# One front program for layer norm, gates and context keys and values, and the spread of the keys moved into the output product

## The reference

```python
x = x + attn(layernorm(x))              # gated delta rule, 16 heads of 128
x = x + xattn(layernorm(x), ctx)        # cross attention to 4 x 64 context rows, 16 heads of 32
x = x + ffn(layernorm(x))               # self attention and two of eight experts
```

```python
# attn: gates of every token and head
g    = exp(-exp(A_log) * softplus(x @ Wa.T + dt_bias));   beta = sigmoid(x @ Wb.T)
# ... recurrence over the tokens, RMS norm, gate by silu(x @ Wg.T), then
out  = o @ Wo.T
# xattn: all 256 context rows serve as keys and values of all queries
kv   = cond @ Wkv + bkv;   k, v = kv[:, :, 0], kv[:, :, 1]
k    = _fq_sym(k, axis=-1)      # rounded to 127 steps of the largest of each key and head
v    = _fq_sym(v, axis=2)       # rounded to 127 steps of the largest of each column
attn = _fq_unsigned(softmax(q @ k.T));   out = (attn @ v) @ Wp + bp
```

## Time and profile before

| what | us |
|---|---|
| median of 3 runs | 3815.62 (3815.4 to 3816.27) |
| the profiled execution, its own time | 3817.35 |
| its span, from first to last instruction | 3815.6 |
| PE busy | 3332.3 (87%) |
| DVE busy | 2142.5 (56%) |
| ACT busy | 1866.6 (49%) |
| POOL busy | 1576.9 (41%) |

### The profile page before, as it was taken

One profiled execution on the slowest core, in us unless ns is written; L12 is line 12 of the kernel. 1 busy time (PEld: TensorE's weight loads), 2 busy tenths in 40 slices (PEclk: granted clock), 3 DMA queues, 4 the chain that ended last, 5 costly groups with the idle time before them and its releaser, 6 DMA issues. The chain is left out here.

```text
span 3815.6 us, 61633 instructions
## 1 busy us (share of the span) xinstructions
PE 3332.3 (87%) x19300; PEld 2601.2 (68%) x19300; DVE 2142.5 (56%) x4562; ACT 1866.6 (49%) x4568; POOL 1576.9 (41%) x3055
## 2 busy tenths in 40 slices
PE   3699999999999999997993888699979999964993
PEld 1588888888888888886772444488746666653441
DVE  3476677666767776765225777555354654621223
ACT  2467776777677766774111555344343533530110
POOL 2577777777777777773001000255530000003103
PEclk7799999999999999998996999899989999975996
DMA  2222222222222222223344000133362022044325
GB/s 51 78 63 67 70 54 70 62 70 65 65 66 71 65 62 70 69 52 100 116 127 169 9 14 14 51 104 110 102 244 89 11 77 71 16 146 156 119 94 157
DMA packets 432119, 311.55 MB, mean 82 GB/s; under 512 B 131392, under 2 KB 348608, under 8 KB 430816
## 3 DMA queue, kind: packets, MB, share of 16 engines
q1 hardware_dynamic: 424544, 288.99, 25.4%
q0 software_dynamic: 5120, 16.78, 1.4%
q10 hardware_dynamic: 2304, 4.20, 0.3%
HBM read 195.99 MB, written 113.90 MB: 81 GB/s over the span
## 5 line engine op out<-in xcount | busy, mean ns | idle before, releaser
L534 PE MATMUL gd_PJ<-xn_lead,gd_w_rest 128*128 128x512 f32 x1024 | 421.4, 411 | 0.0
L534 PE MATMUL gd_PJ<-xn_lead,gd_w_lead 128*128 128x512 f32 x1024 | 403.0, 394 | 0.0
L534 PE MATMUL gd_PJ<-xn_rest,gd_w_lead 128*128 128x512 f32 x1024 | 401.3, 392 | 0.0
L977 POOL TENSOR_TENSOR gd_T<-gd_T,gd_prod 32x14 f32<-32x14 f32 (+6 forms) x896 | 314.2, 351 | 70.2
L974 POOL TENSOR_TENSOR gd_prod<-gd_L,gd_T 32x14 f32<-32x14 f32 (+6 forms) x896 | 285.2, 318 | 70.2
L699 DVE SCALAR_TENSOR_TENSOR gd_conv<-gd_pre,gd_cur_a,gd_conv 128x512 f32<-128x512 f32 x384 | 301.7, 786 | 9.1 <-ACT gd_conv L858 2.3
L2523 POOL MEMSET ms_rank<- 128x1 f32 x8 | 0.3, 98 | 559.2 <-POOLq L55 559.2
L534 PEld LDWEIGHTS gd_PJ<-xn_lead,gd_w_lead 128*128 128x128 f32 x1024 | 193.4, 189 | 43.8
L534 PEld LDWEIGHTS gd_PJ<-xn_lead,gd_w_rest 128*128 128x128 f32 x1024 | 194.2, 190 | 37.4
L534 PEld LDWEIGHTS gd_PJ<-xn_rest,gd_w_lead 128*128 128x128 f32 x1024 | 194.5, 190 | 35.3
L2297 ACT ACTIVATE sa_E<-sa_B,sa_nmax 128x512 f32<-128x512 f32 (+3 forms) x256 | 132.4, 525 | 151.5 <-DVE sa_nmax L2347 151.5
(11 more groups left out here) (403 smaller groups left out, 8905.7 us busy)
## 6 DMA issues: line engine op xcount, KB each, us to landing
turned_queries_keys<-f_wq SPq DMA_DIRECT2D x16, 1280.0 KB, 6.0
gd_row_sums<-decay_sums SPq DMA_DIRECT2D x64, 256.0 KB, 3.7
triangles<-gd_Lo SPq DMA_DIRECT2D x64, 256.0 KB, 3.4
gd_W<-turned_image SPq DMA_DIRECT2D x64, 256.0 KB, 2.8
gd_T<-inverse_image SPq DMA_DIRECT2D x64, 256.0 KB, 3.3
gated_outputs<-gd_og SPq DMA_DIRECT2D x64, 256.0 KB, 2.7
go_ogt<-gated_outputs SPq DMA_DIRECT2D x16, 1024.0 KB, 6.8
sa_qT<-turned_queries_keys SPq DMA_DIRECT2D x16, 1024.0 KB, 5.6
```

The costliest lines, as they stand in the source:

```text
L534: mm = pe.matmul(bank, w_parts[wp][:, j, k, :], rhs, start=(k == 0 and wp == 1), stop=(k == KT - 1 and wp + xp == 0))
L977: nc.gpsimd.tensor_tensor(T16[:, rows, 0:j], T16[:, rows, 0:j], prod[:, rows, 0:j], ALU.subtract).then_inc(solving, 1)
```

## The change

1. `front` takes the place of the layer norm and gates blocks: one block. Tiles of x, the normalised tiles and statistics are double (`xt[:, b % 2]`). The products of the gates, their transposes, the context's transposes, the key product and the value products are put between the transposes of x in PE's list. DVE takes the gates of batch b-1 after normalising batch b, then rounds the keys, then the last gates, then the values. ScalarE copies the turned context after batch 2. SP loads also the context, Wkv in two halves, its biases and the first head's weights `wraw`. Rounded keys `kf`, value integers `vi` and value scales `vs` stay in SBUF through the head stage.
2. `delta_heads` loads only three blocks of 128 constant columns, and no first weights.
3. `delta_out` turns keys and values on PE before it turns Wo. POOL sets `kbd` to zero, spreads the three parts of the keys and scales Wp. Wp and Wq are loaded behind Wo.
4. `cross_setup` becomes `cross_stats`: loads of x first, statistics of each batch as it lands, two biases.

The core of the diff:

```diff
-        xt = sb("xt", [P, CH, DIM])
+        xt = sb("xt", [P, 2, CH, DIM])
...
+            load_x(0)
+            sp.dma_start(cst[:, :], const_dram[:, 0:3 * P]).then_inc(cst_in, 16)
+            load_x(1)
... (Wa, Wb, A_log, dt_bias, ones)
+            sp.wait_ge(xn_done, CH)
+            load_x(2)
+            sp.dma_start(cx[:, :, :], ctx_dram.rearrange("(t p) d -> p t d", p=P)).then_inc(cx_in, 16)
+            sp.dma_start(wkv[:, :, 0:DIM], w_halves[:, :, 0:DIM]).then_inc(wk_in, 16)
+            sp.wait_ge(xn_done, 2 * CH)
+            load_x(3)
+            sp.dma_start(wkv[:, :, DIM:2 * DIM], w_halves[:, :, DIM:2 * DIM]).then_inc(wv_in, 16)
... (biases, seven parameter loads, four loads of wraw)
         @block.tensor            # front; turn_x waits for xn_done, gates for copied, turn_gates for ab_copied
+            turn_x(0)
+            gates(0)
+            turn_x(1)
+            turn_gates(0)
+            gates(1)
+            turn_x(2)
+            turn_gates(1)
+            gates(2)
... (8 transposes of the context)
+            turn_gates(2)
+            pe.wait_ge(wk_in, 16)
+            pe.wait_ge(cxT_ready, 2)
... (key product: 2 x KT matmuls of 128x512)
+            turn_x(3)
+            pe.wait_ge(wv_in, 16)
+            values(0)
+            gates(3)
+            turn_gates(3)
+            for g in range(1, GR):
+                values(g)
             pe.wait_ge(tab_done, 1)
+            pe.wait_ge(kf_taken, 1)
...
         @block.scalar            # front, for each batch b
+                act.wait_ge(var_done, (b + 1) * CH)
+                nc.scalar.activation(std[:, b % 2], mv[:, b % 2, :, 1], ACT.Sqrt, bias=eps[:, 0:1]).then_inc(std_done, 1)
... (for each k: wait turned, copy to xnT, copy to parts[0])
+                if b == 2:
+                    for h in range(2):
+                        act.wait_ge(cx_turned, h + 1)
+                        nc.scalar.copy(cxT[:, 2 * h:2 * h + 2, :], Z[4 + h][:, :].rearrange("p (k n) -> p k n", k=2)).then_inc(cxT_ready, 1)
...
         @block.vector            # front
+            def take_gates(b):
+                dve.wait_ge(ab_done, b + 1)
...
+                nc.vector.tensor_copy(ab[:, :], psAB).then_inc(ab_copied, 1)
+                dve.wait_ge(ab_turned, b + 1)
+                nc.vector.tensor_copy(abt[:, b], psA).then_inc(abt_copied, 1)
... (for each b: statistics, reciprocal after std_done, four normalised tiles)
+                if b == 0:
+                    dve.wait_ge(w_turned, 1)
+                    nc.vector.tensor_copy(wabT[:], psW).then_inc(w_copied, 1)
+                else:
+                    take_gates(b - 1)
+            dve.wait_ge(k_sum, KTL)
... (keys: bias, largest, scale, rounding)
+            take_gates(B - 1)
... (log gates; value bias and largest; sums; row sums; beta; value rounding)
-            sp.dma_start(cst[:, :], const_dram).then_inc(cst_in, 16)
-            load_weights(0)
+            for j, col in enumerate((C_ID, C_GT, C_LV + 64 * MERGE_AT)):
+                sp.dma_start(cst[:, j * P:(j + 1) * P], const_dram[:, col:col + P]).then_inc(cst_in, 16)
+            sp.sem_inc(w_in, 64)
...
         # delta_out
+            sp.dma_start(wp[:, :, :], X["Wp"].rearrange("(g p) n -> p g n", p=P)).then_inc(xw_in, 16)
+            sp.dma_start(wq[:, :, :], X["Wq"].rearrange("(k p) n -> p k n", p=P)).then_inc(xw_in, 16)
...
+        @block.gpsimd
+        def _(pool):
+            for part in range(3):
+                nc.gpsimd.memset(kbd[:, part], 0.0).then_inc(zeroed, 1)
+            pool.wait_ge(zeroed, 3)
+            pool.wait_ge(kT_ready, 2)
+            for part in range(3):
+                if part > 0:
+                    pool.wait_ge(reduced, part * GH)
+                for j in range(GH):
+                    rows = slice(j * XD, (j + 1) * XD)
+                    nc.gpsimd.tensor_copy(kbd[rows, part, :, j * KEYS:(j + 1) * KEYS], kT[rows, :, :]).then_inc(part_ready, 1)
+                if part < 2:
+                    pool.wait_ge(part_ready, part * GH + GH)
... (four subtractions kT - kbd, 32x1024 each, then_inc(reduced))
+            pool.wait_ge(xw_in, 32)
+            for g in range(GR):
+                nc.gpsimd.tensor_tensor(wp[:, g, :], wp[:, g, :], vs[:, g:g + 1].to_broadcast([P, DIM]), ALU.mult).then_inc(scaled, 1)
...
         @block.tensor
             pe.wait_ge(cst_in, 16)
... (8 float32 transposes of kf)
+            tr.then_inc(k_turned, 1)
+            pe.wait_ge(ident_ready, 1)
... (8 bfloat16 transposes of vi with identb)
+            tr.then_inc(v_turned, 1)
             for j in range(KT):
                 pe.wait_ge(wo_in[j], 16)
...
         @block.vector
             nc.vector.reciprocal(rs[:], rs[:]).then_inc(rs_ready, 1)
+            dve.wait_ge(cst_in, 16)
+            nc.vector.tensor_copy(identb[:, :], ident[:, :]).then_inc(ident_ready, 1)
+            dve.wait_ge(k_turned, 1)
+            for h in range(2):
+                nc.vector.tensor_copy(kT[:, 2 * h:2 * h + 2, :], psK[h][:, :, :]).then_inc(kT_ready, 1)
+            dve.wait_ge(v_turned, 1)
+            nc.vector.tensor_copy(vq[:], psV[:, :, :])
...
         # cross_stats
-                dve.wait_ge(x_in, 16 * B)
+                dve.wait_ge(x_in[b], 16)
                 for t in range(b * CH, (b + 1) * CH):
-                    then(nc.vector.bn_stats(stats[:, t, :], xres[:, t, :]))
+                    nc.vector.bn_stats(stats[:, t, :], xres[:, t, :]).then_inc(stat, 1)
```

More of the change, by code:

```diff
@@ L1724, in _, with stage_xattn @@
             add(TILES - 1, TILES // 2 - 1, 1)
[L1727 to L1728 removed]
+def stage_xattn(nc, X, x_dram, const_dram, wq, wp, kbd, vq, bqb, bpb, ahead, out_dram):
     with ExitStack() as ctx:
```

500 lines of the change are left out of this document (228 added, 272 removed).

## The result

The changed kernel takes 3750.52 us (median; 3745.62 to 3754.66), the one before 3815.51 beside it: ratio 0.9829, 95% interval 0.9812 to 0.9846, 65 us less. The forecast was 3751.5.

A forecast was written before the change was run, and what follows sets the result against it. It took the head loop as TensorE-bound and left alone, with the removable time in four barrier-closed stretches no engine fills; -15.6 -5.0 +5.8 +1.5 -51.0 = -64.3 us against 3815.62 was given as 3751.5, range 3743 to 3762.

The forecast's parts named there:

- Cross setup, -51.0: Cross setup: only x's loads and statistics remain, so the stage takes 18.3 us against 69.3; bounds -53 to -48.
- Head stage, -5.0: Head stage start: first weights already in SBUF, first weight turn at +3.3 us instead of +8.4; bounds -5.1 to -2.
- Front, -15.6: Layer norm and gates merged into one block: 79.3 us against 94.9; bounds 74 and 87.
- gates(0): 18.1 to 21.7 at the fast price 3.62: Front: TensorE makes the first batch's gates while waiting for the next normalised batch, in 3.62 us.
- Rival C: Front: TensorE stays at the 1.2 GHz level, slowing gates, key product, values and sums; +16.6 us, 3768; chance 0.08.
- Output product, +5.8 and +1.5: Output product: Wo's turn starts at 1795.5, not 1789.7, behind DVE's identb cast (+5.8); gated rests slowed by POOL (+1.5).
- rival A: Output product: the port lock is let go at each memset's end, so +5.8 becomes 0 or 2.6; 3745.7; chance 0.2.
- +1.5 for the gated rests: Output product: DVE's rests of gated outputs, two SBUF operands, are stretched beside POOL's spread; from 0 to 10 us, taken +1.5.
- Wp and Wq ahead of the first tile: Output product: their 2 MB delays the first gated outputs 5.2 us, to 1806, needed about 1815; costs nothing, at most 5.2.
- Rival B: Output product: gated rests wait for runs of four POOL instructions; +10 us for +1.5, 3760; chance 0.11.
- Rival D: Output product: POOL's slow copies and subtractions end the stage, at 15 us each at about 2101; 3855; chance 0.02.
- The rest, 0: Cross tiles and the three later stages, which the change does not touch: forecast difference 0.

The follow-up runs named there:

- E6: The kernel before, with only the cross setup reordered: x loaded right after the constants, its statistics ahead of the rounding; 3812.82 us, ratio 0.9994.
- E1: The changed kernel with the first head's four weight blocks again loaded at the head stage's start, not in the front; 3752.62 us, ratio 0.9842.
- e10: The changed kernel again, nothing edited, to see scatter; 3745.61 us, ratio 0.9825.
- e7: The changed kernel with 28 extra transposes that nobody reads, in TensorE's gaps in the front; 3744.67 us, ratio 0.9823.
- e4: The changed kernel with the front reordered: x's fourth batch turned and gated before the key product, keys rounded after the log gates; 3739.89 us, ratio 0.9805.
- e2: The changed kernel with POOL waiting for each of its three memsets of kbd before issuing the next; 3741.51 us, ratio 0.9811.
- e5: The changed kernel without POOL's twelve casts into kbd and eight subtractions (output wrong, only times used); 3744.72 us, ratio 0.9824.
- e12: The kernel of e11 with Wp and Wq loads issued by POOL behind its memsets, not by SP ahead of the gated outputs; 3735.38 us, ratio 0.9783.
- e11: The changed kernel with identity cast by ScalarE, front reordered and filled, plus three unread transposes behind each group of four of Wo; 3727.17 us, ratio 0.9782.

## Why the prediction was right, point by point

**Cross setup, -51.0: -51.4.** Right as worked out: the statistics of the four batches, one behind the other. They began 5.7 us into the stage (forecast 5.2) and came 2.7 us apart (2.83), so they ended at 16.5 (16.6). E6 shows that the order of loads and statistics alone gives 3 us of it.

**Head stage, -5.0: -5.9.** Right in mechanism. The first weight turn came at +2.8, not +3.3 (before +8.4). SP's issue of the second row of decay sums came 11.7 us into the stage for 17.3, and POOL's chain on it 15.9 for 21.6: it shifted whole, by 5.7. E1 puts 6.3 us back.

**Front, -15.6: -13.1, and -15.7 in e10.** The order of waits was as walked: turns of x at 13.16, 23.71, 33.70 and 57.48 for 13.0, 22.3, 31.7 and 54.5; log gates at 73.2 for 69.5; end 80.8 for 77.5. The step mis-sized is "gates(0): 18.1 to 21.7 at the fast price 3.62", and the like for the next two: they took 5.42, 5.32 and 5.32, so 1.8, 1.7 and 1.7 us more, in the profiled run. The first turn of x that forecast and run disagree on is exactly the one after the slow batch. In e10 and e7, where the first two batches were fast, the forecast's times came; between e10 and the profiled run of the same program lie 2.6 us of the front, which is the whole miss. Rival C had the right place and named 1.8 and 1.3 us for these two steps, but it also slowed the key product by 4.8, the last gates, the values and the sums. The key product took 8.83 (forecast 9.0), the last gates 3.62, 24 values 5.45 (5.3) and the sums 0.6 to 0.7 each. It was given as all or nothing; it should have been a term for each gap. POOL's rests beside the rounding of keys stretched its last three steps by 2.5 us (5.66 for e4's 3.15), but the last gates' product ended at 65.83 only and VectorE came to it at 66.82, so the path paid 0.95, where 0.8 was put in. The tail from the log gates to VectorE's last step took 7.6 for 8.0.

**Output product, +5.8 and +1.5: +5.8 in all.** The first part was right: Wo's first turn at +11.4 (forecast 11.5), which is 5.6 later than before, for the reason given. The run of memsets was not broken at a boundary, so rival A falls, and e2 shows its condition. Of the +1.5 for the gated rests, the spread's own share is 1.2, in the first rest (e5). Clock added 1.0 in the first tile, and the transposes of Wo took 0.6 less than before. Up to the first finished tile that makes 7.2 of 7.3 us, the last two by chance. The 15 tiles after it then took 1.5 us less than before, and the prediction had no term for that. Some 1.2 of it is the second tile, 11.4 us for 12.6: x's transfer for the third tile took 8.0 us to landing before and in e6, and 6.8 to 7.0 in every kernel with the change. That the one makes the other is likely but not tested, and e12's second tile took 12.7 all the same. Wp and Wq ahead of the first tile cost nothing, as forecast: it landed 23.0 us in and was first read at 30.5. Rival B falls: eight rests were stretched, to 2.63 us at most, but none waited for a run of four, since VectorE got in after each one of POOL's instructions. Rival D is far off: POOL was done 48.6 us into the stage, just below the range of 50 to 70. (By its own numbers, POOL done at 2101 and a stage that else ends at 2007, D's time is about 3846 and not 3855.)

**The rest, 0: -4.9** of one profile against one profile, scatter by the count above. The median hit 3751.5 by 1 us, and part of that is luck. The sum gives 3815.62 - 64.3 = 3751.3, not 3751.5. The errors by stage, +2.5 in the front, -0.9, -1.5, -0.4 and -4.9, went both ways and leave -5.2 of profile against profile. The profiled executions then lay 1.7 us above their median before and 2.7 below it after, which takes most of that back; the repeat gave 3745.61.

## What to carry to other kernels

Before a large memset on POOL is put at a stage's start, look for a VectorE instruction from SBUF to SBUF that TensorE waits for: give it to ScalarE, or make POOL wait for a semaphore between its memsets; either was worth 7 us here. In a ring whose TensorE gaps are a microsecond or so, do not price products at full clock; price both, or fill the gaps with transposes nobody reads. When one wait is removed, read which transfer was just covered by it, as e11 did with the first tile's.

## What the runs showed of the hardware that was not expected

- A run of ready memsets on POOL kept VectorE's cast out for the whole run (8.67 us over two boundaries), and a semaphore wait of POOL's let it in at the first boundary (1.76 us). Beside ready subtractions and casts of POOL's, VectorE got in at every boundary (rests of 1.52 to 2.63 us for 0.69).
- Beside POOL's subtractions, VectorE's operations on 1024 elements from SBUF were stretched even with one tensor operand (1.64 us for 0.69), while beside its memsets copies from PSUM kept 0.65.
- The same program had its early products at 1.2 GHz in one execution and at 2.4 in the next; 28 transposes that nobody reads, in gaps of 1.2 to 2 us, made them fast in 12 of 12, for 5 of 24 without.
- In the cross tiles, where TensorE is busy for about 80% of the time, its clock was at 1.2 GHz in 7 to 12 stretches of 360 us, most of 3.4 us and at about 1 us each; inside the stage each began when TensorE had just been idle for about half of the time or more.
